# Slot attention's scan: the products of neighbouring blocks' decays taken on VectorE instead of GpSimd

## The reference, cut to what matters

```python
def step(carry, xs):
    Sk, Sv = carry
    q_t, k_t, v_t, w_t, g_t, b_t = xs
    gt = jnp.exp(g_t)
    bw = b_t[:, :, None] * w_t
    Sk = Sk * gt[:, :, None, :] + k_t[..., :, None] * bw[:, :, None, :]
    Sv = Sv * gt[..., None] + bw[..., None] * v_t[:, :, None, :]
    s = jnp.einsum('bhd,bhdm->bhm', q_t, Sk) * SCALE
    a = jax.nn.softmax(s, axis=-1)
    o_t = jnp.einsum('bhm,bhmd->bhd', a, Sv)
```

## Time and profile before

| | us |
|---|---|
| median of 3 runs | 2605.76 |
| lowest, highest | 2604.42, 2606.11 |
| the profiled execution, its own time | 2609.29 |
| its span in the trace | 2607.4 |

### The profile page before, as it was taken

How to read it: one execution, slowest core, us unless ns; L and a number is a source line. 1 busy time by engine, 2 the same in 40 slices (tenths; PEclk the granted TensorE clock), 3 DMA queues, 4 the chain that set the end, 5 groups by cost and what they waited for, 6 DMA issues and landing times. The chain is left out here.

```text
span 2607.4 us, 49048 instructions
## 1 busy us (share of the span) xinstructions
PE 2329.5 (89%) x18400; PEld 1615.0 (62%) x18400; DVE 1677.2 (64%) x3286; ACT 1191.4 (46%) x2936; POOL 1100.7 (42%) x1265
## 2 busy tenths in 40 slices
PE   7888888888888888888759999999889989999999
PEld 4577655776557865577635666676533356666685
DVE  7667686677766767677536777742357567777613
ACT  5655455554555545555324555432115535455411
POOL 0477434774347743377525544420130035444300
PEclk9999999999999999999879999998889989999999
DMA  2100001000010000000012000000100030000000
GB/s 63 37 2 3 2 17 37 2 2 2 17 37 2 2 2 17 17 3 2 2 52 74 15 19 19 7 1 1 50 1 1 1 115 19 19 19 13 1 1 17
DMA packets 57640, 46.29 MB, mean 18 GB/s; under 512 B 11576, under 2 KB 50880, under 8 KB 57024
## 3 DMA queue, kind: packets, MB, share of 16 engines
q1 hardware_dynamic: 57408, 43.16, 5.7%
HBM read 42.10 MB, written 1.05 MB: 17 GB/s over the span
## 5 line engine op out<-in xcount | busy, mean ns | idle before, releaser
L1182 DVE SCALAR_TENSOR_TENSOR work<-four,taps,work 128x511 f32<-128x511 f32 (+2 forms) x384 | 285.4, 748 | 101.6 <-ACT work L861 92.0
L1807 POOL TENSOR_TENSOR rot<-q_plain,ropes 128x512 f32<-128x512 f32 x64 | 81.0, 1266 | 577.0 <-ACT q_plain L1838 577.0
L931 ACT ACTIVATE work<-four 128x512 f32<-128x512 f32 x216 | 129.0, 597 | 270.1 <-PE four L690 243.8
L576 PE MATMUL four<-xT,wring 128*128 128x512 f32 x512 | 252.2, 620 | 0.2 <-DVE work L1182 0.2
L741 PE MATMUL four<-work 128*128 128x128 f32 x1536 | 217.2, 286 | 0.0
L1851 ACT ACTIVATE pr<-four,nmaxf 128x512 f32<-128x512 f32 (+3 forms) x256 | 134.0, 525 | 171.2 <-DVE nmaxf L1689 171.2
L1689 DVE TENSOR_REDUCE nmaxf<-four 128x1 f32<-128x512 f32 (+3 forms) x256 | 125.8, 491 | 125.7 <-PE four L1532 121.7
L741 PEld LDWEIGHTS four<-work 128*128 128x128 f32 x1536 | 193.5, 196 | 4.0
L1530 PE MATMUL four<-rot,rot 128*128 128x512 f32 (+3 forms) x512 | 179.0, 445 | 5.2 <-DVE rot L1681 3.6
L1117 POOL TENSOR_TENSOR work<-work 128x256 f32<-128x256 f32 x184 | 146.5, 796 | 77.5 <-DVE work L1263 56.1
L1124 POOL TENSOR_TENSOR work<-work 128x256 f32<-128x256 f32 x184 | 141.9, 771 | 84.0 <-PE bank L775 74.0
(11 more groups left out here) (276 smaller groups left out, 5429.3 us busy)
## 6 DMA issues: line engine op xcount, KB each, us to landing
wqkv<-in_f_wq_dram SPq DMA_DIRECT2D x32, 128.0 KB, 2.2
wqkv<-in_f_wk_dram SPq DMA_DIRECT2D x32, 128.0 KB, 2.4
wqkv<-in_f_wv_dram SPq DMA_DIRECT2D x32, 128.0 KB, 2.3
wo<-in_f_wo_dram SPq DMA_DIRECT2D x2, 2048.0 KB, 11.7
we<-in_f_we_dram SPq DMA_DIRECT2D x4, 1024.0 KB
wring<-in_Wk_dram SPq DMA_DIRECT2D x4, 512.0 KB, 3.8
wring<-in_Ww_dram SPq DMA_DIRECT2D x4, 512.0 KB, 5.5
wring<-in_Wv_dram SPq DMA_DIRECT2D x4, 512.0 KB, 3.9
```

Of the source, the lines that this page charges most:

```text
L576: last = nc.tensor.matmul(unit_bank(i)[:], wring[n % 2][:, c, h * P:(h + 1) * P], k.xT[:, c, b * T:(b + 1) * T], start=(c == 0), stop=(c = ...
L1182: ins = nc.vector.scalar_tensor_tensor(out=cbuf[i % 4][:, n:], in0=unit_bank(i)[:, 0:T - n], scalar=taps[:, {"q": 0, "k": 1}.get(kind, 2), ...
```

## The change

`widen` moves from POOL's program to DVE's, with its waits and its chain `chain_e`. On POOL the calls are deleted, and `decay_keys` and `decay_reach` wait at each level l from 1 on for the join that made `blocks(s, l)`. On DVE one `widen` stands at the head of each half-step j, ahead of that half-step's other calls: levels 0 to 3 of new at j = 3 to 6, levels 4 to 6 of now at j = 0 to 2. `decay_slots` gets no wait of its own. Two waits for the decay tile (`gated`) are added on DVE.

```diff
-                    e = Chain(pool, chain_e, g, B * CH * LEVELS)
-
-                    def widen(s, l):
-                        if l == 0 and s >= 3:
-                            pool.wait_ge(pair_made, order(PAIRS, g, s - 3, LEVELS - 1))
-                        if l == LEVELS - 1 and s >= 3 and keeps_state(s - 3):
-                            pool.wait_ge(pair_used, order(PAIRS, g, s - 3, "state 1"))
-                        eb = blocks(s, l).rearrange("p h (b s) -> p h b s", s=2)
-                        e.then(nc.gpsimd.tensor_tensor(blocks(s, l + 1), eb[:, :, :, 0], eb[:, :, :, 1], ALU.mult))
+                    def decays_there(s, l):
+                        if l:
+                            pool.wait_ge(chain_e, (g * SLOTS + s) * LEVELS + l)
...
+                        decays_there(s, l)
                         src = U if l else chunk(wT, s)
...
+                        decays_there(s, l)
                         src = S[s % 3] if l else chunk(gT, s)
...
                             if j == 4 and new is not None:
-                                widen(new, 0)
                                 decay_keys(new, 0)
-                                widen(new, 1)
                             if now is not None and (now, j + LAG) in CHAIN_W:
                                 decay_keys(now, j + LAG)
-                            if now is not None and j + LAG + 1 < LEVELS:
-                                widen(now, j + LAG + 1)
...
                                 decay_keys(new, j - 4)
-                                widen(new, j - 3)
...
+                    dve.wait_ge(gated, g * 8 + HG)
+                    e = Chain(dve, chain_e, g, SLOTS * LEVELS)
+
+                    def widen(s, l):
+                        if l == 0 and s >= 3:
+                            dve.wait_ge(pair_made, order(PAIRS, g, s - 3, LEVELS - 1))
+                        if l == LEVELS - 1 and s >= 3 and keeps_state(s - 3):
+                            dve.wait_ge(pair_used, order(PAIRS, g, s - 3, "state 1"))
+                        eb = blocks(s, l).rearrange("p h (b s) -> p h b s", s=2)
+                        e.then(nc.vector.tensor_tensor(blocks(s, l + 1), eb[:, :, :, 0], eb[:, :, :, 1], ALU.mult))
...
                         for j in range(LEVELS):
+                            if s == 0 and j == 0:
+                                dve.wait_ge(gated, g * 8 + 8)
+                            if j == 3 and new is not None:
+                                widen(new, 0)
+                            if j == 4 and new is not None:
+                                widen(new, 1)
+                            if j > 4 and new is not None:
+                                widen(new, j - 3)
+                            if now is not None and j + LAG + 1 < LEVELS:
+                                widen(now, j + LAG + 1)
                             if j == 3 and mid is not None:
                                 first_values(mid)
```

More of the change, by code:

```diff
@@ L1149, in _ @@
                                 decay_slots(old, j + 4)
-                    e.end()
             @block.vector
@@ L1364, in _ @@
                     ch.end()
+                    e.end()
 WORK_WORDS = 12672
```

## The result

The changed kernel takes 2657.91 us (median of 4 runs, 2653.81 to 2663.45) against 2605.94 of the kernel before beside it: ratio 1.0209, 95% interval 1.0190 to 1.0228. It is 52 us slower. The sign was forecast; the size was not: 12 us were forecast, with 2633 as the upper end. The profiled execution took 2657.26 us, its span is 2655.5.

What follows compares the result with a forecast made beforehand. DVE was taken as co-bound of the full steps, through its dense stretch. Step terms summed to +3.5 us a group, taken as +3, so +12 us over four groups: forecast 2617.5 us, range 2594 to 2633.

Steps and rivals of the forecast that it cites:

- dense stretch: In a full step, DVE's run without a gap from its release by PE to the end of line 1301, 15.1 us.
- POOL is the bound: Rival, chance 0.23: PE's waits for POOL shrink in full steps, 4.8 us a group gained, 2587 us.
- DVE dearer than thought: Rival, chance 0.1: joins wait for POOL's work to end, +8 to +10 us a group, 2640 us.
- D: Time five joins add to the dense stretch: 1.38 plus 0.65 interference less 0.3 given back, 1.7 us; bounds 1.1 and 2.4.
- the interference: POOL stretching DVE's joins in the dense stretch: 0.13 us for each join, 0.65 for five.
- that wait of PE stays about as it is: PE's wait for POOL at 561.38, 1.25 us: POOL's gain of about 0.5 us is lost by DVE's 0.7.
- the slack: 0.79 us in step 5 between line 1301's signal and PE's need of it; taken off D in steps 4 to 6.
- Step 7: Only the joins of levels 4 to 6, 1.1 us less the slack: +0.2 us a group.
- Step 2: No slack, but some 0.4 us of small idle times at the dense stretch's start: 1.7 - 0.4 = +1.3 us.
- Step 0: POOL loses five joins, 2.2 us, and DVE has idle time for them: -2.2 us a group.
- Levels 1 and 2 hidden: Joins at j = 4 and 5 lie before DVE's release, where it sat idle 1.82 us, so they cost nothing.
- POOL's new waits: POOL's waits for DVE's joins: cheap, as each level is joined two half-steps before POOL reads it; should not bind.

Runs made afterwards that it cites:

- experiment 1: The kernel before with no joins at all: POOL's join line taken out, DVE given none, output not the reference's; 2593.81 us, ratio 0.9972.
- experiment 12: The changed kernel with levels 3 to 6 as product-reduces and levels 0 to 2 still two-input products; 2614.45 us, ratio 1.0039 to the kernel before.
- experiment 5: The changed kernel with every join written as a product-reduce over pairs, one SBUF input, same place and waits; 2610.38 us, ratio 1.0036 to the kernel before.
- experiment 10: The kernel before with only the joins of slots 0 and 1 on DVE, as product-reduces, the others on POOL; 2597.32 us, ratio 0.9964.
- experiment 6: The kernel before, joins kept on POOL, with two-input copies of them on DVE that POOL's lines 1105 and 1117 wait for; 2627.06 us, ratio 1.0106.
- experiments 4: The changed kernel with all seven joins of the next slot moved to half-steps 4 and 5, where DVE waited; 2631.36 us, ratio 1.0120 to the kernel before.
- experiment 8: The kernel before with levels 2 to 6 joined on DVE at half-step 5 as two-input products, levels 0 and 1 on POOL; 2627.76 us, ratio 1.0107.

## Why the prediction was right or wrong, point by point

The second group, step by step, from PE's pair product to the next (step 0: from POOL's second key product of slot 0 to its second of slot 1; step 1: from there on):

| step | 0 | 1 | 2 | 3 | 4 | 5 | 6 | 7 | sum |
|---|---|---|---|---|---|---|---|---|---|
| forecast | -2.2 | -0.2 | +1.3 | +1.7 | +0.9 | +0.9 | +0.9 | +0.2 | +3.5 |
| measured | -1.2 | -0.2 | -0.4 | +2.7 | +3.4 | +2.9 | +2.3 | +3.5 | +13.0 |

- *What bounds*: right in the main. DVE's dense stretch has no slack in steps 2 and 3, experiment 1 shows that POOL's relief moves no full step, and experiment 12 that the stretching inside it is what costs.
- *The sign and the rivals*: right to have slower; the rival "POOL is the bound" (2587) falls by experiment 1. The rival "DVE dearer than thought" (2640, chance 0.1) named the right mechanism and was given too small a chance. Its D, 2.5 to 3, holds the measured 2.65; its time fell short by the second term below.
- *The term that failed*: the interference, 0.13 us for each join, taken from the mean excess of lines 1266 and 1297, and the 0.3 given back. Measured, the seven joins of a slot take 3.47 us; undisturbed 1.5 to 1.6 by the fastest rows of their kind, so the excess is 0.27 each. In step 3 the five joins of the stretch take 2.32, where the sum had 1.13 and 0.65 for POOL; nothing was given back, and D was 2.65, not 1.7. Line 1314 (after: 1316) rose from 0.525 to 0.640 in the mean. Line 1299 fell by 0.21, not because POOL interferes less but because the join now stands in front of it until POOL's instruction is over; with the reduces of experiment 5, of 0.69 us, it is as short. The mistake was to take the excess as a share of a like instruction. It is what is left of POOL's running instruction, up to 0.6 us, whatever DVE's own size; a small one pays it in full.
- *Where the agreement would be luck*: with the interference taken away (experiment 5) the sum's 12 lies near the measured 9. But D is 1.07 there and not 1.7, because the reduces take 1.38 and about 0.5 really is given back; the nearness of the two totals says little.
- *The second term*: the sum stopped at the stretch's end. It held that "that wait of PE stays about as it is" and named no wait of PE on lines 1314 and 1290. With D at 2.65 both come into play (33.7 and 36.5 us in the profile of after, 12.1 and 22.7 before), PE idles 3.3 us in three pieces and in steps 4, 5 and 7 its clock falls after them. Steps 4 to 6 therefore lost 3.4, 2.9 and 2.3 us where D less the slack gives 1.9.
- *Step 7*: the sum counted three joins in it. The one of level 3 stands behind DVE's release too (620.36), so there are four, 1.55 us.
- *Step 2*: +1.3 forecast. Its stretch did grow by that much, from 14.63 to 15.97, but the step got shorter: before, PE's granted clock was 0.90 over this step (0.70 in the first 7 us), after it was 1.00. The gain comes from the clock, which the sum didn't look at; in the first group the step grew by 1.9.
- *Step 0*: -2.2 forecast. The change took 465.42 - 451.03 = 14.39 us against 455.91 - 440.36 = 15.55: -1.2. Five of the seven joins in it are stretched there too (0.46 to 0.77); by product-reduce for slots 0 and 1 alone (experiment 10) it took 449.16 - 435.40 = 13.76, -1.8, and the gain shows in the time, 8 us.
- *Levels 1 and 2 hidden*: right, by experiment 12.
- *POOL's new waits*: they cost nothing, by experiment 6, but they aren't all met early: that POOL waits for the joins was named as a sign of being wrong, and it does, a little. The waits of the change put 28 of POOL's waits, 22.3 us, down to joins. At the 20 before line 1113 it is line 1265 that ends them in truth: at 512.48 the join had ended at 511.89, line 1265 at 512.34, and POOL starts 0.14 behind that line, as it did behind line 1263 before the change. The 8 before line 1100, 4.2 us, are real.
- *The other signs*: the step was to be 25.6 us long and the waits for line 1301 25 us or more; measured 26.6 to 28.2, and 18.7 us.

## What to carry to other kernels

Before moving small work from POOL to DVE, look at the highest duration of DVE's like instructions, not at the mean: with two SBUF inputs each can pay for the rest of POOL's running instruction, which for a small one is several times its own price. A pairwise product written as a reduce over the pairs has one SBUF input and didn't pay it. One input alone is no safeguard, though: a `TENSOR_SCALAR` and a `COPY` of this kernel paid it too (below). And ask where DVE's queue has no gap: stretching cost nothing under the idle time of levels 1 and 2, and most in the dense stretch; but idle time is to be read step by step, as experiments 4 and 8 (31 and 26 us over) show.

## What the runs showed of the hardware

- An elementwise product of DVE from two SBUF inputs of four elements took 0.17 us (experiment 8, all 32) or 0.58 us (the change, all 32), there ending 0.02 to 0.03 us after POOL's running instruction. The one of 256 elements ended 0.28 us after it, in all 28 stretched executions.
- Not only two inputs: in the kernel before, line 1284, with one SBUF input of four elements, ended 24 to 28 ns after POOL's instruction in 24 of 32 executions, and line 1296, a copy, 0.15 us after it in 15 of 32. The line's durations, lowest, median, highest:

```profile
L1284 DVE TENSOR_SCALAR nmax<-nmax x32: 170/440/454, 135.2 to 1280.0; 128x4 f32<-128x4 f32 x32
```

- Not stretched in any execution of the change: line 1253, a product of a PSUM bank with an SBUF mask (409 to 426 ns in all 160), and the reduces of line 1285 (676 to 692). The product-reduce of 512 elements took 685 to 689 ns in all 32 executions of experiment 5.
- A product-reduce over pairs costs by its input: 686 ns for 512 elements read, 415 for 256, 206 for 64, 153 for 8.
- PE's granted clock fell from the upper of its two levels (2.4 GHz) to the lower (1.2) at the end of the three idle times of step 4 (1.14, 1.59 and 0.57 us) in the change; the next eight matmuls of line 741 took 1.91 us instead of 1.06. After the same three in step 6 it stayed up.
